# Query, key and value projections regrouped over the engines, a threshold search with experts on partitions, and a gate kept on chip

## The chip, the cores and the metric

The kernel runs on one core of a Trainium2 chip. Its time is device microseconds (us) of one execution, and lower is better. The core has five instruction streams that run side by side and meet at semaphores: TensorE (PE, with its weight loads as PEld), VectorE (DVE), ScalarE (ACT), GpSimd (POOL) and SyncE (SP), which issues most DMAs. Each takes its own instructions in order.

## The reference, cut to what matters

Four pre-norm layers on 4 x 1024 tokens of width 128, in fp32. The parts that the change touches are the two attentions' projections, the routing of the second feed-forward layer and the gated state-space layer:

```python
# L0: q, k = x @ Wq + bq, x @ Wk + bk; 16 heads of 8; rotary: x*cos + rot(x)*sin; v = x @ Wv + bv; softmax attention
# L1 attention: q, k, v = x @ w_qkv.T, no bias, no rotary
# L1 feed-forward: top-1 of 8 experts with a capacity
logits = tokens @ router_w.T
probs = softmax(logits); top1_idx = argmax(probs); top1_prob = max(probs)
order = lexsort((-top1_prob, top1_idx))          # by expert, most probable first
keep = place in the expert's group < capacity    # the others go to expert 0
# L3: state-space layer
xp, z, Bp = split(x @ Win, 3)
...                                              # causal conv of xp, silu, scan -> y
yn = (y - mu) / sqrt(var + 1e-5) * ln_g + ln_b
x = x + (yn * sigmoid(z)) @ Wout * res_scale
```

## The kernel before

The kernel is a row of stages, one function each. A stage allocates its tiles, opens a block with one instruction list per engine, and ends where all engines meet, so the stages' lengths add up. The activations stay on the chip, transposed: 128 features on partitions and 4096 tokens in 8 chunks of 512.

**Projections** (`qkv_stage`, run as `a0_qkv` with biases and rotary, `rope`, and as `a1_qkv` without). It works through 16 items, k = 0 to 15: the query of a chunk (even k) and its key (odd k). Every fp32 result is split into three bf16 parts whose sum is the value: high, the rounded rest, and the rest of that. With rotary an item takes these steps: PE multiplies twice (L408: once plain, once with rotated weights); DVE adds the bias and multiplies with the cosine table, then the same with the sine table (L429, into `t1` and `t2`); POOL adds the two (`full`, L363, semaphore `summed`); ACT rounds it (`high`, L464, into `part[0]`); DVE subtracts (`remain`, L436, into `rest`); ACT rounds the rest (`middle`, L468, `part[1]`); POOL subtracts again (`lo`, L351, `part[2]`); and SP stores the three parts to the DRAM stacks `a_qstk` and `a_kstk` (L379), with three DMAs for a query and four for a key, 128 KB each. The lists interleave items: ACT does `high(k)`, then `middle(k-2)`; POOL `full(k)`, then `lo(k-2)`. Without rotary ACT rounds from PSUM and POOL only does `lo`. The tiles are rings of four items: `high(k)` and `lo(k)` wait until the stores of item k-4 have landed (`stored`). After item 5's stores, SP also fetches the head pairs 0, 1 and 2 of batch 0 back from the stacks, in the forms that attention reads (`fetch_stacks`, four DMAs for each of two heads, L318 to L321): one head after each of items 5 to 10. POOL begins with eight memsets of 32 x 1024 ones (L356).

**Attention** (`attention_stage`) takes 64 head pairs over both layers' batches, fetched by POOL one pair ahead; its first two pairs begin with row maxima alone (PE L604, DVE L693).

**Top-1 routing** (`top1_stage`, `f1r`) needs each expert's capacity-th probability. It searches for it in 14 rounds of base 4 (`dve.Fori`, L1608 to L1626): DVE makes three tries per expert (L1609), compares 128 tokens x 3 x 8 x 32 (L1612), adds up over the tiles (L1615), PE adds over the partitions (L1559), and DVE takes the step (L1617 to L1625). Between the rounds PE turns two tiles of tokens for other use. GpSimd's padding of the gate's weights (L845, L847) comes before the first product of the stage.

**The state-space layer**: `conv_in_stage` writes z to DRAM (L1908), `ssm_stage` scans, `norm_stage` with k = 2 (`m3n`) normalizes, and `ssm_out_stage` (`m3o`) reads z back (L2503), takes its sigmoid (ACT L2511), applies gain and bias (DVE L2521), multiplies (L2526), projects (PE L2541) and adds the result (DVE L2529), in a loop over chunks with two buffers; each chunk's add stands before the next chunk's gain and multiplication on DVE.

## Time and profile before

| | |
|---|---|
| median of three runs | 3428.6 us (3421.51, 3428.60, 3431.22) |
| the profiled execution | 3450.99 us |
| its span, first to last instruction | 3449.3 us |
| PE / DVE / ACT / POOL busy | 78% / 72% / 53% / 29% |
| mean granted TensorE clock | 0.896 |
| `a0_qkv`, `a1_qkv` | 75.2 us, 56.5 us |
| `f1r` | 94.7 us |
| conv, scan, norm, out of the state-space layer | 57.4, 57.6, 38.8, 52.7 us |

Times are microseconds from the start of the span unless marked ns, "x" is a count, and L12 is line 12 of the kernel. An idle time names what ended it. Since a stage ends where all engines meet, a busy share of the whole span tells little here: what counts is, inside a stage, which chain of engines repeats, and how long one turn of it takes.

### The profile page before, as it was taken

How to read it: one execution, taken by the hardware profiler on the slowest of the kernel's cores; microseconds unless marked ns; L12 is line 12 of the kernel's file. 1: busy time of each engine (PE TensorE's matmuls, PEld its weight loads, DVE VectorE, ACT ScalarE, POOL GpSimd, SP SyncE). 2: the span in 40 equal slices, each digit the busy share in tenths (PEclk: the TensorE clock that was granted, in tenths of full speed). 3: DMA queues.
4: the chain of work that ended last, by engine and by line, in shares of the span. 5: the costliest groups of instructions: out<-in, count | busy, mean ns of one | idle time of the engine just before them, and what ended most of it. 6: DMA issues, size and time to landing. Idle time of an engine off the chain costs nothing. (4 is left out here: it accounts for less than half of the span.)

```text
span 3449.3 us, 43078 instructions
## 1 busy us (share of the span) xinstructions
PE 2678.1 (78%) x12690; PEld 960.5 (28%) x12690; DVE 2495.4 (72%) x2926; ACT 1819.0 (53%) x3161; POOL 1003.2 (29%) x1205
## 2 busy tenths in 40 slices
PE   7599999984477669999997418767777778996666
PEld 3122222221155412222221107422232323332222
DVE  6799999954155389999994541579999964446548
ACT  2388888882033248888887104355555531224233
POOL 4222222200635212222220026236777730000000
PEclk9699999997799869999999658888999988998778
DMA  3111111106222311111110402101000000001010
GB/s 95 53 29 24 24 27 23 26 11 153 48 72 65 112 40 24 28 23 24 27 23 23 127 18 70 61 28 39 13 7 13 6 0 0 0 0 60 12 37 25
DMA packets 165673, 128.54 MB, mean 37 GB/s; under 512 B 65341, under 2 KB 138941, under 8 KB 165296
## 3 DMA queue, kind: packets, MB, share of 16 engines
q1 hardware_dynamic: 129520, 85.31, 9.5%
q0 software_dynamic: 34880, 37.57, 4.0%
q10 hardware_dynamic: 1152, 4.19, 0.3%
q8 instruction: 58, 0.95, 0.1%
q14 instruction: 63, 0.52, 0.0%
HBM read 72.80 MB, written 54.09 MB: 37 GB/s over the span
## 5 line engine op out<-in xcount | busy, mean ns | idle before, releaser
L693 DVE TENSOR_REDUCE a_att_mx<-a_att_s 128x2 f32<-128x1024 f32 x1024 | 1204.5, 1218 | 60.1 <-PE a_att_s L604 47.4
L678 ACT ACTIVATE a_att_pt<-a_att_st 128x512 f32<-128x512 f32 x2048 | 1064.5, 603 | 233.3 <-PE a_att_st L630 232.6
L630 PE MATMUL a_att_st<-a_qst,a_kst 50*128 50x512 bf16 x2048 | 623.0, 385 | 62.9 <-ACT a_att_pt L678 51.5
L604 PE MATMUL a_att_s<-a_kst,a_qst 48*128 48x512 bf16 x2048 | 527.1, 400 | 78.1 <-PEq L344 45.2
L617 PE MATMUL a_att_av<-a_att_pt,a_att_vst 128*32 128x512 f32 x4096 | 547.7, 607 | 0.0
L630 PEld LDWEIGHTS a_att_st<-a_qst,a_kst 50*128 50x128 bf16 x2048 | 158.9, 94 | 727.2 <-ACT a_att_pt L678 668.7
L2256 POOL TENSOR_TENSOR g_xn<-m2s_hs,m2s_cb 128x1024 f32<-128x1024 f32 x128 | 300.9, 2356 | 119.0 <-DVE m2s_hs L2223 69.8
L2223 DVE TENSOR_TENSOR_SCAN m2s_hs<-m2s_da,m2s_bps 128x1024 f32<-128x1024 f32 x128 | 292.7, 2287 | 4.4
L531 POOL CAST a_att_mt_in<-a_att_nmax 128x16 bf16<-128x16 f32 x64 | 12.6, 196 | 936.7 <-DVE a_att_nmax L701 936.7
L2139 PE MATMUL m2s_yps<-g_xn,g_ident 128*128 128x512 f32 x512 | 243.8, 599 | 0.9
L2195 ACT COPY m2s_cb<-m2s_cps 128x1024 f32<-128x1024 f32 x128 | 129.5, 1012 | 184.1 <-POOL g_xn L2256 182.1
L604 PEld LDWEIGHTS a_att_s<-a_kst,a_qst 48*128 48x128 bf16 x2048 | 113.1, 94 | 230.9 <-DVE a_att_mx L693 169.9
L2218 DVE TENSOR_TENSOR m2s_bps<-m2s_dtx,m2s_bps 128x1024 f32<-128x1024 f32 x128 | 154.7, 1209 | 3.9 <-POOL m2s_dtx L2242 3.9
L164 POOL MEMSET n_mean_w<- 128x128 f32 x8 | 1.6, 204 | 521.6 <-POOLq L982 232.3
L2190 ACT ACTIVATE m2s_da<-m_dt,m2s_aneg 128x1024 f32<-128x1024 f32 x128 | 147.4, 1151 | 0.0
L2159 PE MATMUL m2s_bps<-m_bcs,m2s_sel 96*128 96x512 bf16 x256 | 79.7, 394 | 83.9 <-DVE m2s_hs L2223 81.3
L1024 ACT ACTIVATE f_sg<-f_gp 128x512 f32<-128x512 f32 x72 | 43.0, 597 | 181.2 <-PE f_cp L1013 181.2
L1036 DVE TENSOR_TENSOR f_h<-f_sg,f_up 128x512 f32<-128x512 f32 x72 | 49.5, 687 | 121.6 <-ACT f_sg L1024 121.6
L2139 PEld LDWEIGHTS m2s_yps<-g_xn,g_ident 128*128 128x128 f32 x512 | 97.2, 191 | 85.6 <-issue 64.1
L617 PEld LDWEIGHTS a_att_av<-a_att_pt,a_att_vst 128*32 128x32 f32 x4096 | 81.0, 108 | 129.8 <-issue 102.6
L271 ACT ACT_TABLE_LOAD x9 | 11.5, 1283 | 183.3 <-PEq L751 64.7
L1258 POOL DMA_INDIRECT f_back<-f_yr,f_to x78 | 74.7, 958 | 88.1 <-DVE f_yr L1452 66.6
(479 smaller groups left out, 3777.7 us busy)
## 6 DMA issues: line engine op xcount, KB each, us to landing
a_kstk<-a_qkv_part SPq DMA_DIRECT2D x64, 128.0 KB
f_xs<-f_sent SPq DMA_DIRECT2D x20, 396.0 KB, 6.1
a_qst<-a_qstk POOLq DMA_DIRECT2D x116, 64.0 KB, 2.3
a_kst<-a_kstk POOLq DMA_DIRECT2D x116, 64.0 KB, 2.4
a_qstk<-a_qkv_part SPq DMA_DIRECT2D x48, 128.0 KB, 2.2
f_sent<-f0r_zero SPq DMA_DIRECT2D x1, 5148.0 KB, 21.9
a_num<-a_att_oev SPq DMA_DIRECT2D x256, 16.0 KB
g_xn<-a_num ACTq DMA_DIRECT2D x8, 512.0 KB, 5.8
```

The source lines that it names most:

```text
L604: mm = pe.matmul(s1[:, cut % 2, h, :], qst[u][64 * h:64 * h + SPECIAL, qt * P:(qt + 1) * P], kst[u][64 * h:64 * h + SPECIAL, kh * CH:(kh + ...
L617: mm = pe.matmul(av[32 * gr:32 * gr + 32, :], vst[u][:, kt, h, :], pt[:, 4 * (kt % 4) + 2 * half + h, :], start=kt == 0, stop=kt == 7)
L630: pe.matmul(st[:, e % 3, :], kst[u][64 * h:64 * h + STACK, kt * P:(kt + 1) * P], qst[u][64 * h:64 * h + STACK, half * CH:(half + 1) * CH], ...
L678: act.activation(pt[:, e % 16, :], st[:, e % 3, :], ACT.Exp, scale=scale).then_inc(exp_done, 1)
L693: dve.tensor_reduce(mx[:, par, 2 * cut:2 * cut + 2], s1[:, cut % 2, :, :], AX.X, ALU.max).then_inc(s1_used, 1)
L2139: mm = pe.matmul(yps[:, f, :], g.ident[:, :], hc[:, k % 4, f * CH:(f + 1) * CH], start=n == 0, stop=n == NS - 1)
L2159: mm = pe.matmul(bps[:, k % 2, f, :], sel[:, n:n + 1].to_broadcast([96, P]), bcs[:, (2 * (q // 2) + f) * CH:(2 * (q // 2) + f + 1) * CH], ...
L2190: act.activation(da[:, k % 4, :], dt[:, q % 2, span(q)], ACT.Exp, scale=aneg[:, q % 2, n:n + 1]).then_inc(da_done, 1)
L2195: act.copy(cb[:, k % 2, :], both(cps[:, :, :])).then_inc(c_copied, 1)
L2218: dve.tensor_tensor(over, dtx[:, q % 2, :], over, ALU.mult).then_inc(dbx_done, 1)
L2223: dve.tensor_tensor_scan(hs[:, k % 3, :], da[:, k % 4, :], over, 0.0, ALU.mult, ALU.add).then_inc(scan_done, 1)
L2256: pool.tensor_tensor(hc[:, k % 4, :], hs[:, k % 3, :], cb[:, k % 2, :], ALU.mult).then_inc(hc_done, 1)
```

## The change

**Projections.** The cosine product is written back into its PSUM bank (L434), and DVE adds it and `t2` (`total`, L447) in POOL's place. With rotary POOL does the first remainder as well as the last (`remain`, L357; `last`, L363). ACT takes `middle(k-1)` ahead of `high(k)`. The three parts lie in one tile, in an order in which a query goes out as one DMA of 128 x 3 x 512 and a key as three. SP fetches head pair 0 only, after item 7, both heads at once; pairs 1 and 2 are fetched by POOL at the start of attention, ahead of its memsets. POOL's first memsets are four of 128 x 1024.

**Threshold search.** The probabilities are turned so that a partition holds one expert and 16 of the tiles (two transposes, one copy); a round is one add, three comparisons of 128 x 256 that accumulate on the way, one product with a matrix that joins the partitions of an expert, one counting comparison and one update, written out 14 times. The 42 offsets are set by GpSimd memsets of 128 x 1 ahead of everything else in the stage.

**State-space layer.** z stays in SBUF (`m3_gate`, 32 KB per partition); its sigmoid is taken at the end of `ssm_stage`; the gain moves into the normalization's last product (`gain`); `ssm_out_stage` is written out for 8 chunks, with two instead of four DVE instructions per chunk ahead of the add, four PSUM banks, and the add two chunks behind.

```diff
-Q_PARTS = [(1, slice(0, HD)), (0, slice(HD, 2 * HD)), (2, slice(2 * HD, 3 * HD))]
-K_PARTS = [(0, slice(0, 2 * HD, 2)), (1, slice(1, 2 * HD, 2)), (2, slice(2 * HD, 3 * HD)), (0, slice(3 * HD, 4 * HD))]
+Q_MOVES = [(slice(0, 3), slice(0, 3 * HD))]
+K_MOVES = [(slice(1, 2), slice(0, 2 * HD, 2)), (slice(0, 1), slice(1, 2 * HD, 2)), (slice(1, 3), slice(2 * HD, 4 * HD))]
...
+                def remain(k):
+                    pool.wait_ge(hi_done, k + 1)
+                    if k >= 4:
+                        pool.wait_ge(lo_done, k - 3)
+                    pool.tensor_tensor(rest[:, k % 4, :], full[:, k % 4, :], hi(k), ALU.subtract).then_inc(rest_done, 1)
...
-                    for h in range(2):
-                        pool.memset(t[64 * h + 32:64 * h + 64, :], 1.0).then_inc(ones_set, 1)
-                pool.wait_ge(ones_set, 8)
+                    pool.memset(t[:, :], 1.0).then_inc(ones_set, 1)
+                pool.wait_ge(ones_set, 4)
+                for k in range(ITEMS):
+                    if rope:
+                        remain(k)
+                        if k >= 1:
+                            last(k - 1)
...
+                        if n == 1:
+                            sp.dma_start(stacks[k % 2][rows, :, cols(k // 2)], part[:, k % 4, parts.start, :]).then_inc(stored[k % 4], 16)
+                        else:
+                            sp.dma_start(stacks[k % 2][rows, :, cols(k // 2)].rearrange("(p r) h t -> (r h) p t", r=HD),
+                                         part[:, k % 4, parts, :]).then_inc(stored[k % 4], 16)
+                    if k == 7:
+                        sp.wait_ge(ones_set, 4)
...
+                        for h in range(2):
+                            fetch_stacks(sp, stacks, qst[0], kst[0], 0, 0, h, first_here)
...
+                    dve.wait_ge(prod, 2 * k + 1)
+                    dve.scalar_tensor_tensor(out=bank(k, 0), in0=bank(k, 0), scalar=col[("bq", "bk")[k % 2]][:, :],
+                                             in1=cos[:, tok], op0=ALU.add, op1=ALU.mult).then_inc(by_cos, 1)
...
+                def total(k):
+                    dve.wait_ge(by_cos, k + 1)
+                    dve.wait_ge(by_sin, k + 1)
+                    if k >= 4:
+                        dve.wait_ge(rest_done, k - 3)
+                    dve.tensor_tensor(full[:, k % 4, :], bank(k, 0), t2[:, k % 2, :], ALU.add).then_inc(summed, 1)
...
@@ attention_stage, POOL
+                for hp in (1, 2):
+                    for h in range(2):
+                        fetch_stacks(pool, stacks, qst[hp], kst[hp], 0, hp, h, ldq[hp])
                 for u in range(4):
                     pool.memset(vst[u][:, :, :, :], 0.0).then_inc(vset, 1)
@@ top1_stage, POOL
+                for k in range(bits):
+                    for j in range(3):
+                        pool.memset(offsets[:, k, j:j + 1], 0.25 ** (k + 1) * (j + 1)).then_inc(offsets_set, 1)
+                pool.wait_ge(offsets_set, 3 * bits)
                 pool.wait_ge(w.here, w.all)
                 found.pad(pool)
@@ top1_stage, PE
+                    pe.wait_ge(counted_here, 3 * (k + 1))
+                    pe.matmul(cnt_ps[:, 0:3], same_w[:, :], parts[:, :], start=True, stop=True).then_inc(counted, 1)
...
+                pe.wait_ge(thr_done, bits + 1)
+                pe.transpose(turned_thr, own_thr[:, :].to_broadcast([P, P]), g.ident[:, :]).then_inc(thr_turned, 1)
@@ top1_stage, DVE
+                for k in range(bits):
+                    dve.wait_ge(thr_done, k + 1)
+                    dve.tensor_scalar(tries[:, :], offsets[:, k, :], own_thr[:, :], None, ALU.add).then_inc(tries_done, 1)
+                    dve.wait_ge(tries_done, k + 1)
+                    for j in range(3):
+                        dve.tensor_scalar(above[:, j, :], by_expert[:, :], tries[:, j:j + 1], None, ALU.is_ge, ALU.add,
+                                          accum_out=parts[:, j:j + 1]).then_inc(counted_here, 1)
                     dve.wait_ge(counted, k + 1)
...
@@ ssm_stage, ACT, its end
+                for b in range(BATCH):
+                    for i in range(2):
+                        z = gate[:, i, b * SEQ:(b + 1) * SEQ]
+                        act.activation(z, z, ACT.Sigmoid).then_inc(opened, 1)
@@ ssm_out_stage, DVE
+                        dve.scalar_tensor_tensor(out=yg[:, c % 4, i, :], in0=yn[:, i, cols(c)], scalar=lb[:, i:i + 1],
+                                                 in1=gate[:, i, cols(c)], op0=ALU.add, op1=ALU.mult).then_inc(gated, 1)
...
+                for c in range(NCH):
+                    weigh(c)
+                    if c >= 2:
+                        add(c - 2)
```

Where the instructions stand, in the changed kernel's lines for "after". First VectorE in `a0_qkv`, from item 4 (`a0_qkv_ps` is the projection in PSUM, `area0` the weights, biases and tables, `a0_v` the values). Before:

```order
L429 SCALAR_TENSOR_TENSOR a0_qkv_t1<-a0_qkv_ps,area0 128x512
L429 SCALAR_TENSOR_TENSOR a0_qkv_t2<-a0_qkv_ps,area0 128x512
L436 TENSOR_TENSOR a0_qkv_rest<-a0_qkv_full,a0_qkv_part0 128x512
L429 SCALAR_TENSOR_TENSOR a0_qkv_t1<-a0_qkv_ps,area0 128x512
L429 SCALAR_TENSOR_TENSOR a0_qkv_t2<-a0_qkv_ps,area0 128x512
L419 TENSOR_TENSOR a0_v<-a0_qkv_v,area0 128x512
L436 TENSOR_TENSOR a0_qkv_rest<-a0_qkv_full,a0_qkv_part0 128x512
```

After:

```order
L434 SCALAR_TENSOR_TENSOR a0_qkv_ps<-a0_qkv_ps,area0 128x512
L439 SCALAR_TENSOR_TENSOR a0_qkv_t2<-a0_qkv_ps,area0 128x512
L447 TENSOR_TENSOR a0_qkv_full<-a0_qkv_ps,a0_qkv_t2 128x512
L434 SCALAR_TENSOR_TENSOR a0_qkv_ps<-a0_qkv_ps,area0 128x512
L439 SCALAR_TENSOR_TENSOR a0_qkv_t2<-a0_qkv_ps,area0 128x512
L447 TENSOR_TENSOR a0_qkv_full<-a0_qkv_ps,a0_qkv_t2 128x512
L427 TENSOR_TENSOR a0_v<-a0_qkv_v,area0 128x512
```

The remainder, which had both inputs in SBUF, is gone from VectorE; a sum with one input in PSUM stands in its place, directly behind the products it adds. GpSimd's list at the same place read `full`, last remainder, `full`, last remainder; it now reads first remainder of k, last remainder of k-1.

Second, VectorE in `f1r`, one round of the search and what stands before it (`f1r_pm` the probabilities by token, `f1r_cnt` the counts in PSUM). Before, in a loop:

```order
L1603 SCALAR_TENSOR_TENSOR f_block_k<-g_ones 128x23
L1604 TENSOR_SCALAR f1r_count_k<-f_block_k 128x23
L1608 UNCONDITIONAL_BRANCH
L1609 TENSOR_TENSOR f1r_tries<-f1r_inc,f1r_thr 128x24
L1611 REGISTER_ALU
L1612 TENSOR_TENSOR f1r_above<-f1r_pm,f1r_tries 128x768
L1615 TENSOR_REDUCE f1r_parts<-f1r_above 128x24
L1617 SCALAR_TENSOR_TENSOR f1r_passed<-f1r_cnt,f1r_inc 128x24
L1621 TENSOR_REDUCE f1r_step_sum<-f1r_passed 128x8
L1624 TENSOR_SCALAR f1r_inc<-f1r_inc 128x24
L1625 TENSOR_TENSOR f1r_thr<-f1r_thr,f1r_step_sum 128x8
L1608 REGISTER_ALU
```

After, written out:

```order
L1631 SCALAR_TENSOR_TENSOR f_block_k<-g_ones 128x23
L1632 TENSOR_SCALAR f1r_count_k<-f_block_k 128x23
L1633 MEMSET f1r_own_thr 128x1
L1636 COPY f1r_by_expert<-f1r_gate_row 128x256
L1640 TENSOR_SCALAR f1r_tries<-f1r_offsets,f1r_own_thr 128x3
L1643 TENSOR_SCALAR f1r_above,f1r_parts<-f1r_by_expert,f1r_tries 128x256 x3
L1646 TENSOR_SCALAR f1r_passed,f1r_passes<-f1r_cnt 128x3
L1649 SCALAR_TENSOR_TENSOR f1r_own_thr<-f1r_passes,f1r_own_thr 128x1
```

The comparison of 768 elements and the separate reduction have become three instructions of 256 elements, and four small ones have become two.

## Rows read from the trace of the kernel before

**Rows 1.** Windows: length, then busy us (count) of PE, PEld, DVE, ACT, POOL, granted clock, DMA share, GB/s.

```profile
35.60:110.80 75.20, 40.41 (x128) 20.93 (x129) 45.07 (x56) 18.24 (x33) 51.02 (x41) 0.80 0.37 112
110.80:148.00 37.20, 20.75 (x72) 3.57 (x73) 36.55 (x35) 2.55 (x5) 3.68 (x13) 0.50 0.03 8
190.00:500.00 310.00, 297.58 (x2012) 71.47 (x2013) 298.52 (x284) 268.95 (x520) 79.05 (x176) 1.00 0.11 26
1161.90:1218.40 56.50, 26.85 (x96) 15.81 (x96) 15.84 (x24) 17.58 (x32) 25.83 (x24) 0.71 0.48 149
3268.20:3320.90 52.70, 26.22 (x32) 8.10 (x32) 23.08 (x40) 13.14 (x12) 0.00 (x0) 0.63 0.23 80
```

**Rows 2.** Waits in `a0_qkv`, 35 to 111 us: total, times, longest.

```profile
ACT a_qkv_part L464 <- POOL a_qkv_full L363: 53.0, 14, 18.5
```

**Rows 3.** Timeline of `a0_qkv`: start, us, engine, line, operation, count, idle before.

```profile
35.65 7.93 POOL L356 MEMSET a_kst<- 32x1024 bf16 x8 [20.90 <-POOLq L156]
...
39.48 0.75 DVE L429 SCALAR_TENSOR_TENSOR a_qkv_t<-a_qkv_ps,area 128x512 f32<-128x512 f32 x1 [0.87 <-PE a_qkv_ps L408]
...
43.67 2.50 POOL L363 TENSOR_TENSOR a_qkv_full<-a_qkv_t 128x512 f32<-128x512 f32 x2
...
44.97 1.41 DVE L429 SCALAR_TENSOR_TENSOR a_qkv_t<-a_qkv_ps,area 128x512 f32<-128x512 f32 x2 [1.71 <-POOL a_qkv_full L363]
...
62.48 1.71 POOL L363 TENSOR_TENSOR a_qkv_full<-a_qkv_t 128x512 f32<-128x512 f32 x1
...
64.80 0.61 ACT L468 CAST a_qkv_part<-a_qkv_rest 128x512 bf16<-128x512 f32 x1
65.49 1.15 POOL L351 TENSOR_TENSOR a_qkv_part<-a_qkv_rest,a_qkv_part 128x512 bf16<-128x512 f32 x1 [1.30 <-ACT a_qkv_part L468]
65.55 1.64 DVE L436 TENSOR_TENSOR a_qkv_rest<-a_qkv_full,a_qkv_part 128x512 f32<-128x512 f32 x1
```

**Rows 4.** Waits in `a1_qkv`, 1161 to 1219 us.

```profile
ACT a_qkv_part L464 <- DMA a_kstk<-a_qkv_part: 16.7, 6, 4.5
```

**Rows 5.** Timeline of `a1_qkv`, ScalarE: item 4's rounding.

```profile
1173.96 0.58 ACT L464 CAST a_qkv_part<-a_qkv_ps 128x512 bf16<-128x512 f32 x1 [3.84 <-DMA a_qstk<-a_qkv_part]
```

**Rows 6.** The stores' line, L379: issue ns min/median/max, and landing.

```profile
L379 SPq DMA_DIRECT2D a_kstk<-a_qkv_part x64: 427/529/778, 54.2 to 1217.6; - x64
...
DMA to landing us min/median/max: 1.9/2.2/3.3
```

**Rows 7.** Timeline of `f1r`: first try, the step after a count, first row behind the search.

```profile
1956.08 0.18 DVE L1609 TENSOR_TENSOR f1r_tries<-f1r_inc,f1r_thr 128x24 f32<-128x24 f32 x1 [0.20 <-DVE f1r_count_k L1604]
...
1964.47 0.18 DVE L1617 SCALAR_TENSOR_TENSOR f1r_passed<-f1r_cnt,f1r_inc 128x24 f32<-128x24 f32 x1 [0.71 <-PE f1r_cnt L1559]
...
2020.81 0.43 DVE L1628 TENSOR_TENSOR f1r_t<-f1r_pm,f1r_thr 128x256 f32<-128x256 f32 x1 [0.21 <-DVE f1r_thr L1625]
```

**Rows 8.** Groups by line: a tensor-scalar instruction of VectorE; busy, mean ns.

```profile
L1946 DVE TENSOR_SCALAR m3i_acc<-m3i_xb,g_area 128x512 f32 x16 | 7.0, 481 | 4.5 <-ACT m_xs L1965 4.5
```

**Rows 9.** Timeline at the program's start: memsets of one column on GpSimd.

```profile
0.32 0.10 POOL L2813 MEMSET const-bfloat16-1.0<- 128x1 bf16 x1
0.35 0.10 POOL L2813 MEMSET const-uint8-127<- 128x1 uint8 x1
```

**Rows 10.** Timeline of norm `m3n` and of `m3o`, where z is read back.

```profile
3229.66 1.28 ACT L271 ACT_TABLE_LOAD   x1 [13.35 <-PEq L2291]
...
3262.85 4.87 DVE L238 TENSOR_TENSOR m_xs<-m_xs,m3n_row 128x512 f32<-128x512 f32 x8 [2.21 <-PE m3n_row L205]
...
3273.20 1.28 ACT L2511 ACT_TABLE_LOAD   x1 [19.00 <-DMA m3o_zt<-m_z]
3274.49 2.00 ACT L2511 ACTIVATE m3o_sg<-m3o_zt 128x1024 f32<-128x1024 f32 x2
...
3288.08 1.98 PE L2541 MATMUL m3o_ps<-m3o_yg,g_area 128*128 128x512 f32 x4 [2.44 <-DVE m3o_yg L2526]
...
3298.09 3.78 PE L2541 MATMUL m3o_ps<-m3o_yg,g_area 128*128 128x512 f32 x4 [2.44 <-DVE m3o_yg L2526]
```

301 lines of the change are left out of this document (130 added, 171 removed).

## The prediction, as put on record before the changed kernel ran

> **What bounds the kernel now.** I first read the table of windows by stage [rows 1]: stages end where all engines meet, so a saving inside one shortens the whole by as much, and each edit is priced in its own stage. Then, per stage, the waits and the timeline. Attention itself is bound by TensorE at full clock (297.58 of 310.00 us) and its code hardly changes. In `a0_qkv` no engine is busy for more than 51.02 of 75.20 us. The longest wait is ScalarE's for GpSimd's sum, 53.0 us [rows 2]: a loop over engines, to be seen in the timeline [rows 3]. GpSimd's `full` (1.71) releases ScalarE's `high`, `middle` of two items back (0.61) stands behind that, and `lo` (1.15) behind that; only then comes the next `full`: 1.71 + 0.61 + 0.61 + 1.15 with short handoffs is 4.1 us per item, 16 times. In `a1_qkv` ScalarE waits for the landing of stores, for the keys alone 16.7 us [rows 4]. The search runs from 1956.08 to 2020.81 [rows 7], 64.7 us, 4.62 a round, in one chain through DVE and PE. In `m3o` the chain per chunk passes DMA, ACT, DVE, PE and DVE, and little overlaps; ScalarE's first wait there, counted from inside the norm, ends with z's landing at 3273.20, 5 us into the stage [rows 10].
>
> **A: `a0_qkv`.** Per item DVE now does two products (1.41 the pair), a sum (about 0.68, the pair's second half plus the same class as the uncontended remainder) and half a value copy (0.34): 2.4. GpSimd does two remainders. None of its rows is such a first remainder; the nearest are `full` alone, 2.50 for two, so 1.25, and `full` beside a DVE remainder with both inputs in SBUF, 1.71, in which case that remainder takes 1.64 [rows 3]. The DVE pair from PSUM at 44.97 ran inside the 2.50 and neither was stretched. In the changed kernel every DVE instruction of this stage has at most one tensor input in SBUF, as that pair had, so I take 1.25; with `last` at 1.15 that is 2.4. The loop is now first remainder 1.25, `middle` 0.61, `high` 0.61 and three handoffs of some 0.05: **2.6 us per item**; GpSimd's last remainder runs beside ScalarE. PE's 40.41 us make 2.5 an item, partly at the lower clock, so PE is next in line. The sum: the first item's sine product still starts at 39.48; plus 0.75 and the sum 0.69, `high(0)` starts at 41.0. The memsets, 7.93 for eight, halve and end at 39.6, ahead of it. Fifteen turns end at 80.0; the last item's chain is 0.6 + 1.25 + 0.6 + 1.15 and handoffs, 3.9; three key stores at 0.53 to issue [rows 6] 1.8; leaving 0.4. The eight fetches behind item 7, at 0.53 or a little more 4.5 us of SP, hold up item 8's store, for which item 12 waits: its slack is about 2, so 2.5 is added. End at 88.6 instead of 110.8: **-22**. Bounds: remainders at 1.71 with `last` (loop 3.06), -15; loop at the engines' own 2.4 and no hold-up, -28.
>
> **B: `a1_qkv`.** A ring of four items turns through `high` 0.58, remainder 0.69, `middle` 0.61, `lo` 1.15, handoffs 0.3, issue and landing. Issue was three or four DMAs per item plus four fetches, and SP had little air; it is one or three now. Landing was 1.9 to 3.3 [rows 6]; the joined stores carry two or three times the bytes, so I take the upper part: 3.3 + 1.6 + 3.3 is 8.2, **2.0 per item**. Item 4's rounding started at 1173.96 [rows 5]; four memsets less and one query DMA instead of three bring it to 1171. Eleven items later 1193; the eight fetches hold up 4; the last item's chain 3.3, its stores 1.8, leaving 0.4: 1202.8 against 1218.4, **-15.6**. Bounds: 1.7 per item and nothing held up, -23; 2.6 per item, -9.
>
> The fetches of pairs 1 and 2 move to GpSimd at the start of attention: 16 DMAs, some 9 us, ahead of its memsets. All of GpSimd's list queues behind them, and pair 1's row maxima wait for the first eight. In that stretch GpSimd works 3.68 of 37.20 us, while DVE is busy for 36.55 [rows 1] and reaches pair 1 only halfway: zero; without that cover at most 9 per layer.
>
> **C: the search.** A round: tries 0.2; three accumulating comparisons of 256 elements, of which no row exists; the count over PE 0.71 [rows 7]; two small steps 0.44; another 0.05. The nearest row by size is 0.43 for 256 elements in a tensor-tensor instruction [rows 7]; by kind, 0.48 for 512 [rows 8]. I take the former, as accumulation is something extra: three overlapping a little, 1.1. A round is 2.5, fourteen 34.7: 30.0 less. To be paid: turning the threshold back over PE, about 0.71 and two small handoffs, 1.4; the copy of the turned probabilities less four memsets, 0.1; 42 memsets of GpSimd ahead of the padding for which the stage's first product waits: 0.03 apart or 0.10 long [rows 9], 1.4 to 4.2; I take 2.5. **-26**. Bounds: comparisons as by kind (0.3 each), -32; a full second pass in each, as the old compare and reduce, 2.5 for the three, -6.
>
> The Trainium skill, "VectorE: DVE Perf Modes", section on the perf-mode tier table, says that a tensor-scalar instruction on fp32 in SBUF runs at twice the rate of a tensor-tensor one. The 0.48 for 512 elements agrees; whether accumulation keeps the rate no row here shows. By the rule the term would be -32. [...]
>
> **D: the state-space layer.** Eight sigmoids, 2.00 for two and a table load 1.28, take 9.3 us on ScalarE, which idles 13.35 at that place [rows 10]: hidden; without cover up to 9. The normalization's 16 products go from 0.61 to 0.66 each (4.87 for eight; 1.41 for two with a scalar [rows 3]): +1. In `m3o` DVE needs three instructions of 0.66 per chunk, 2.0. PE needs 3.78 per chunk at 1.2 GHz and 1.98 at 2.4 GHz [rows 10]. It enters after a pause, at the lower level; in `a0_qkv` and `a1_qkv`, also entered after a pause, the granted clock came to 0.80 and 0.71 of full speed [rows 1], so it rose early there. So: 1.4 to the first product, 3.8, 2.7 for a chunk that changes over, then six at DVE's pace less the two that wait ready, about 10, and the last add 0.9: 18.8 against 52.7, -34. With the +1, **-33**. The bound is 1.2 GHz throughout: 1.4 + 8 x 3.6 + 0.8, 31, so -21.
>
> **The sum**: -22 - 15.6 - 26 - 33 = -96.6. The profiled execution took 3450.99 us, 22.4 above the median; it would take 3354.4, and the median becomes 3428.6 - 96.6 = **3332 us**.
>
> **Rivals.**
> 1. *Stores bound both projections.* A joined store lands late, since it moves 384 KB where 128 KB took up to 3.3, and the ring waits at every item: A at 3.0, B at 2.6 per item, 6.5 + 6.5 lost: 3345. For: the DMA share was already 0.48 in `a1_qkv`. Against: SP issues far less.
> 2. *`m3o` stays at 1.2 GHz*: 12 lost, 3344. For: it ran mostly there before. Against: it will be fed without pauses.
> 3. *Accumulation costs a second pass*: 20 lost, 3352.
> 4. *Slower than before*: attention loses the clock. DVE has 18 rows a pair, so the 284 rows of the 310 us are 15.8 pairs, 19.6 us each, with PE busy for 96% of it; at 1.2 GHz instead of 2.4 it takes about 19 more. The place is the entry into attention, which PE reaches at 0.50 [rows 1] and from which it must rise; if more than five of the 64 pairs fall short, all that was won is gone, and ten give 3428.6 - 96.6 + 190 = 3522. For: the entry's first pair waits for GpSimd's fetches now. Against: they land long before, and 190 to 500 us shows 1.00.
>
> **How the numbers follow.** The forecast holds 0.70, rival 1 0.10, rival 2 0.09, rival 3 0.06, rival 4 0.05 (0.03 over the line, 0.02 at five pairs, where nothing is left). All lower bounds at once (-28, -23, -32, -33) give 3313, all upper ones (-15, -9, -6, -21) 3378; they are independent, so their squares add: about 11 below and 25 above, and the runs spread by some 5 each way. Range **3314 to 3362**, which takes in rivals 1 to 3 alone. A measurement of this kernel tells about 0.3%, 10 us, from no change: faster 0.95, within 0.02, slower 0.03.
>
> **What would show it.** `a0_qkv` some 53 us with GpSimd rows of 1.25 and 1.15 and one item every 2.6; rows of 1.7 would refute A. In `a1_qkv` some 41 us, ScalarE's waits for landings mostly gone but for one near item 12; rival 1 shows as a wait at every item. In the search a round of 2.5 with comparison rows near 0.4; `f1r` near 69 us. `m3o` near 19 us with a clock above 0.8; rival 2 shows 3.8 per chunk. ScalarE's sigmoids end before DVE's last sum in the scan. The forecast is wrong if the attention windows change by more than a few us, or if a stage not named here moves.

## The result and the profile after the change

| | before | after |
|---|---|---|
| median of runs, us | 3426.2 (3421.5 to 3431.2, 4 runs) | 3328.5 (3326.8 to 3354.9, 4 runs) |
| ratio, 95% interval | | 0.9732 [0.9704, 0.9761] |
| profiled execution / its span | 3450.99 / 3449.3 | 3326.78 / 3325.0 |
| TensorE's granted clock, mean | 0.896 | 0.908 |

The kernel became 98 us faster by the medians, 92 ± 10 us by the ratio; 3332 us were forecast. The profiled executions differ by 124 us, which is more than the change brought: 30.6 us of it lie in the first expert stage, `f0r` and `f0`, whose code is the same in both (below). By stage, from the first instruction of one to that of the next, in us:

| stage | before | after | difference | forecast |
|---|---|---|---|---|
| `a0_qkv` | 75.1 | 52.6 | -22.5 | -22 |
| attention and output, first layer | 702.2 | 703.2 | +1.0 | 0 |
| `f0r`, `f0` (unchanged code) | 305.9 | 275.3 | -30.6 | 0 |
| `a1_qkv` | 56.5 | 43.9 | -12.6 | -15.6 |
| attention and output, second layer | 702.6 | 702.2 | -0.4 | 0 |
| `f1r`, `f1` | 253.1 | 226.8 | -26.3 | -26 |
| `m3s` | 57.8 | 59.6 | +1.8 | 0 |
| `m3n`, `m3o` | 91.5 | 57.5 | -33.9 | -33 |

The four stages that the change speeds up give -95.3, with `m3s` -93.5. The windows of the changed kernel answer to [rows 1]; columns as there, the last row being `m3o`:

```profile
34.67:87.31 52.64, 37.18 (x128) 20.22 (x129) 37.20 (x56) 18.73 (x33) 39.99 (x36) 0.86 0.45 143
87.31:111.00 23.69, 12.74 (x44) 2.27 (x44) 23.01 (x22) 1.48 (x2) 12.45 (x29) 0.50 0.19 51
190.00:500.00 310.00, 297.27 (x2012) 71.64 (x2016) 298.59 (x284) 268.57 (x520) 76.36 (x170) 1.00 0.11 25
1109.86:1153.72 43.86, 24.47 (x96) 14.14 (x96) 15.66 (x24) 17.48 (x32) 21.91 (x20) 0.81 0.54 170
3180.00:3198.92 18.92, 16.68 (x32) 7.03 (x32) 16.23 (x24) 0.00 (x0) 0.00 (x0) 0.83 0.00 0
```

In `a0_qkv` GpSimd is busy 11 us less than in [rows 1] and no engine is busy for more than 40.0 of 52.6 us. In the attention's entry, 87.31 to 111.00, GpSimd works 12.45 us where the kernel before had 3.68 [rows 1]: the 16 moved fetches. DVE stays at 23.01 of 23.69 us there, and from attention's start to ScalarE's first exponential it is 36.0 us in both kernels (110.77 to 146.79, 87.31 to 123.32), so they are hidden, as the step on the fetches had it. Attention itself still has a granted clock of 1.00.

The item of `a0_qkv`, in the timeline of all engines (start, us, engine, line, operation, tiles, count, idle before), TensorE and SyncE left out; it answers to [rows 3]:

```profile
57.68 0.61 ACT L474 CAST a_qkv_part<-a_qkv_full 128x512 bf16<-128x512 f32 x1
...
58.37 1.16 POOL L357 TENSOR_TENSOR a_qkv_rest<-a_qkv_full,a_qkv_part 128x512 f32<-128x512 f32 x1
...
58.69 0.69 DVE L447 TENSOR_TENSOR a_qkv_full<-a_qkv_ps,a_qkv_t 128x512 f32<-128x512 f32 x1
...
59.49 1.15 POOL L363 TENSOR_TENSOR a_qkv_part<-a_qkv_rest,a_qkv_part 128x512 bf16<-128x512 f32 x1
...
59.56 0.62 ACT L478 CAST a_qkv_part<-a_qkv_rest 128x512 bf16<-128x512 f32 x1 [1.27 <-POOL a_qkv_rest L357]
...
60.08 0.61 ACT L474 CAST a_qkv_part<-a_qkv_full 128x512 bf16<-128x512 f32 x1
...
60.77 1.16 POOL L357 TENSOR_TENSOR a_qkv_rest<-a_qkv_full,a_qkv_part 128x512 f32<-128x512 f32 x1
```

From one first remainder (58.37) to the next (60.77) it is 2.40 us, and the way leads through the loop that the forecast named: first remainder 1.16, handoff 0.03, `middle` (59.56), `high` 0.52 behind its start (60.08), 0.61 for `high`, handoff 0.08. It is 2.4 and not 2.6 because the remainder takes 1.16 and not 1.25, and because ScalarE starts `high` 0.52 behind `middle`, not 0.61. GpSimd's last remainder runs beside ScalarE and ends at 60.64, 0.13 before GpSimd may go on. VectorE, with two products, a sum and half a value copy an item, needs 2.4 us as well (its sums start at 53.90, 58.69 and 63.48, two items apart): it is as close to the limit as the loop. The rest of the stage's length is a wait for stores. The waits of ScalarE in the two projections (total us, times, longest), which answer to [rows 2] and [rows 4]:

```profile
ACT a_qkv_part L478 <- POOL a_qkv_rest L357: 20.3, 16, 1.3
ACT a_qkv_part L474 <- DMA a_qstk<-a_qkv_part: 3.8, 1, 3.8
...
ACT a_qkv_part L474 <- DMA a_kstk<-a_qkv_part: 11.4, 6, 3.2
ACT a_qkv_part L474 <- DMA a_qstk<-a_qkv_part: 6.7, 3, 5.7
```

The first two are of `a0_qkv`, the last two of `a1_qkv`. The longest of each stage, 3.8 and 5.7 us, is item 12's wait behind the eight fetches. The other eight in `a1_qkv` are the ring of four.

The search, VectorE's and TensorE's rows of one round; they answer to [rows 7]:

```profile
1896.85 0.23 DVE L1640 TENSOR_SCALAR f1r_tries<-f1r_offsets,f1r_own_thr 128x3 f32<-128x3 f32 x1
1897.12 0.48 DVE L1643 TENSOR_SCALAR_CACHE_REDUCE f1r_above<-f1r_by_expert,f1r_tries 128x256 f32<-128x256 f32 x1
1897.52 0.08 DVE L1643 DVE_READ_ACCUMULATOR f1r_above<-f1r_by_expert,f1r_tries 128x1 f32 x1
1897.52 0.47 DVE L1643 TENSOR_SCALAR_CACHE_REDUCE f1r_above<-f1r_by_expert,f1r_tries 128x256 f32<-128x256 f32 x1
...
1898.46 0.59 PE L1586 MATMUL f1r_cnt<-f1r_parts,f1r_same 128*128 128x3 f32 x2 [1.51 <-DVE f1r_above L1643]
...
1899.48 0.23 DVE L1640 TENSOR_SCALAR f1r_tries<-f1r_offsets,f1r_own_thr 128x3 f32<-128x3 f32 x1
```

A round is 2.63 us (1896.85 to 1899.48; 4.62 before, 2.5 forecast). Each comparison is an instruction of 0.48 us and a read of the accumulator of 0.08, and they start 0.40 apart: 1.28 for the three against the 1.1 of the forecast.

### The profile page after: what moved, and what is told of

It is laid out like the page before. It is cut to its first block and busy times, and to the rows that moved or that the text cites. A ratio compares the mean times of both kernels' runs of the same rounds, so it can differ in the third digit from the quotient of the medians.

```text
span 3325.0 us, 42836 instructions
## 1 busy us (share of the span) xinstructions
PE 2664.8 (80%) x12693; PEld 959.3 (29%) x12693; DVE 2465.1 (74%) x2953; ACT 1815.3 (55%) x3157; POOL 1006.7 (30%) x1271
## 5 line engine op out<-in xcount | busy, mean ns | idle before, releaser
L708 DVE TENSOR_REDUCE a_att_mx<-a_att_s 128x2 f32<-128x1024 f32 x1024 | 1204.8, 1219 | 62.0 <-PE a_att_s L619 49.7
L541 POOL CAST a_att_mt_in<-a_att_nmax 128x16 bf16<-128x16 f32 x64 | 12.6, 198 | 914.6 <-DVE a_att_nmax L716 914.6
```

The source lines that it names most:

```text
L708: dve.tensor_reduce(mx[:, par, 2 * cut:2 * cut + 2], s1[:, cut % 2, :, :], AX.X, ALU.max).then_inc(s1_used, 1)
```

## The experiments

Stages of every kernel's profiled execution, as above, in us; "att" is attention with its output stage:

| kernel | `a0_qkv` | att 1 | `f0` | `a1_qkv` | att 2 | `f1` | `m3s` | `m3n`+`m3o` |
|---|---|---|---|---|---|---|---|---|
| before | 75.1 | 702.2 | 305.9 | 56.5 | 702.6 | 253.1 | 57.8 | 91.5 |
| after | 52.6 | 703.2 | 275.3 | 43.9 | 702.2 | 226.8 | 59.6 | 57.5 |
| after_again | 53.0 | 721.6 | 272.8 | 42.9 | 702.2 | 226.8 | 59.6 | 57.6 |
| proj_only | 54.0 | 719.5 | 274.8 | 43.8 | 711.7 | 251.9 | 59.6 | 87.6 |
| search_only | 75.2 | 702.4 | 276.3 | 56.5 | 721.2 | 226.6 | 59.2 | 93.0 |
| ssm_only | 75.5 | 702.4 | 275.0 | 56.8 | 702.7 | 252.8 | 61.7 | 57.6 |
| cos_in_sbuf | 56.2 | 703.8 | 273.2 | 43.7 | 701.5 | 227.0 | 59.6 | 57.5 |
| stores_apart | 54.3 | 702.4 | 273.7 | 44.7 | 702.0 | 228.0 | 57.8 | 58.7 |
| fetch_spread | 51.2 | 702.7 | 273.6 | 41.2 | 702.6 | 226.4 | 59.6 | 57.6 |
| ring8 | 49.8 | 702.8 | 273.7 | 38.9 | 719.6 | 226.7 | 59.6 | 57.5 |
| ring8_act | 49.7 | 703.8 | 273.8 | 36.7 | 701.1 | 228.0 | 61.9 | 57.7 |
| count_by_reduce | 52.1 | 702.7 | 272.8 | 43.7 | 702.4 | 236.5 | 59.6 | 57.5 |
| add_at_once | 54.8 | 702.1 | 273.8 | 43.0 | 702.1 | 227.0 | 59.6 | 71.0 |
| fill_tail | 49.4 | 703.9 | 273.4 | 38.3 | 703.4 | 226.8 | 59.6 | 57.6 |

Where a stage's code is the same, the table shows its scatter: `a0_qkv` of the changed kernel 52.1 to 54.8, `a1_qkv` 42.9 to 43.9, attention 701 to 704 but 712 to 722 in five of 28 cases, `f0` 273 to 276 in 13 executions and 305.9 in one.

### The three parts alone

**proj_only** has all of the change but the search and the state-space layer, in short:

```diff
+LO, HI, MID = (0, 2), (1, 1), (2, 0)
...
+                    dve.tensor_tensor(full[:, k % 4, :], bank(k, 0), t2[:, k % 2, :], ALU.add).then_inc(summed, 1)
...
+                for hp in (1, 2):
+                    for h in range(2):
+                        fetch_stacks(pool, stacks, qst[hp], kst[hp], 0, hp, h, ldq[hp])
```

> The kernel before with the projections, the joined stores and the moved fetches alone; search and state-space layer as before. Theory 1 (every part acts in its own stage; the 30 us by which the first transformer block's expert layers were shorter in the one profiled execution of the changed kernel are scatter of that execution): a0_qkv near 52.6 and a1_qkv near 43.9 us, attention and its output +1.0 in the first block, 35 us less than before, so about 3391. Theory 2 (the expert stage behind the first attention, whose code is unchanged, is lastingly shorter by some 30 us, and some other part gained that much less): 60 to 65 us less, about 3363, with that stage near 275 us here too.

**search_only** has the search alone:

```diff
+                        dve.tensor_scalar(above[:, j, :], by_expert[:, :], tries[:, j:j + 1], None, ALU.is_ge, ALU.add,
+                                          accum_out=parts[:, j:j + 1]).then_inc(counted_here, 1)
```

> The kernel before with the turned search alone. Theory 1: the routed expert stage falls from 253 to 227 us, all in the search; 26 us less, about 3400; the norm and the expert stages behind it unchanged. Theory 2 (the experts behind the search hide part of it, or another stage moves with it): less than 15 us or more than 35.

**ssm_only** has the state-space layer's change alone:

```diff
+                        act.activation(z, z, ACT.Sigmoid).then_inc(opened, 1)
...
+                        dve.scalar_tensor_tensor(out=yg[:, c % 4, i, :], in0=yn[:, i, cols(c)], scalar=lb[:, i:i + 1],
+                                                 in1=gate[:, i, cols(c)], op0=ALU.add, op1=ALU.mult).then_inc(gated, 1)
```

> The kernel before with the state-space layer's change alone. Theory 1: norm and output stage together 57.5 instead of 91.5 us; m3s between 57.8 and 59.6; 32 to 34 us less, about 3393. If m3s is longer by 1.8 us because of the eight sigmoids, it is 59.6 here too; if that was TensorE's clock at the end of that stage, the rows that grew are matmuls, and m3s may be 57.8 here. Rival (sum right by compensation): the three parts alone add up to less than 85 or more than 110 us.

Measured against the kernel before, whose median was 3436.0 in these comparisons: proj_only 0.9893 [0.9855, 0.9931], search_only 0.9921 [0.9893, 0.9949], ssm_only 0.9879 [0.9848, 0.9911]. By the ratios that is 37, 27 and 42 us less, 106 together, ± 20 when the half intervals are added by squares; the whole change gave 92 ± 10 by its ratio. By the medians it is 40, 33 and 47, or 121, against 98: more than the 110 that the expectation allowed. The kernel before had a median of 3436 in this comparison and of 3421 to 3426 in the others, so the whole times are too coarse to settle the sum. The stages settle it. Against the row of before, proj_only saves 21.1 and 12.7 us in the two projections, search_only 26.5 in `f1`, ssm_only 33.9 in `m3n` and `m3o`: 94.2 together, where the whole change saved 95.3 in these stages. So the parts add up, each in its own stage, and theory 1 holds for all three. The `f0` stage is near 275 us in each of them, in two of which its code and that of all that precedes it is that of the kernel before. The 305.9 us of the profiled execution of before were thus scatter and no gain of the change. They more than account for the 22 us by which that execution stood above its median.

The 1.8 us of `m3s` are not the sigmoids: proj_only, which has none, shows 59.6 too, and stores_apart, which has them, shows 57.8. The granted clock differs, over the whole stage (0.82 where it takes 57.8 us, 0.78 at 59.6, and 0.74 at the 61.7 and 61.9 of ssm_only and ring8_act) and most in its last 24 us. Windows of that stretch, proj_only, then stores_apart (columns as in [rows 1]):

```profile
3171.00:3195.10 24.10, 15.01 (x24) 4.36 (x22) 17.30 (x13) 2.27 (x3) 0.04 (x1) 0.65 0.00 1
```

```profile
3114.00:3137.50 23.50, 13.26 (x29) 4.33 (x28) 18.21 (x14) 11.19 (x11) 0.00 (x0) 0.75 0.00 0
```

ScalarE works 11.19 us in the shorter and 2.27 in the longer one. The sigmoids are hidden, as forecast: in the changed kernel ScalarE still idles 5.81 us before the norm's table load.

### Why the item of `a0_qkv` fell to 2.4 us

**cos_in_sbuf:**

```diff
-            t2, full = s.sb("t2", [P, 2, CH]), s.sb("full", [P, 4, CH])
+            t1, t2, full = s.sb("t1", [P, 2, CH]), s.sb("t2", [P, 2, CH]), s.sb("full", [P, 4, CH])
...
-                    dve.scalar_tensor_tensor(out=bank(k, 0), in0=bank(k, 0), scalar=col[("bq", "bk")[k % 2]][:, :],
+                    dve.scalar_tensor_tensor(out=t1[:, k % 2, :], in0=bank(k, 0), scalar=col[("bq", "bk")[k % 2]][:, :],
...
-                    dve.tensor_tensor(full[:, k % 4, :], bank(k, 0), t2[:, k % 2, :], ALU.add).then_inc(summed, 1)
+                    dve.tensor_tensor(full[:, k % 4, :], t1[:, k % 2, :], t2[:, k % 2, :], ALU.add).then_inc(summed, 1)
```

> The changed kernel, but the cosine product is written to SBUF again, so DVE's sum has both inputs there. Theory 1 (a DVE instruction with two inputs in SBUF and GpSimd's remainders stretch each other, as the two kinds did in the kernel before: 1.71 against 1.25 and 1.64 against 0.69 us): GpSimd's first remainder rises from 1.16 to 1.5 to 1.7, DVE's sum from 0.69 to 1.2 or more, the item from 2.41 to 3.0 or more, a0_qkv from 52.6 to 62 or more; a1_qkv stays at 43.9. Theory 2 (keeping the product in PSUM buys nothing, the loop is shorter only because both remainders stand on one engine and ScalarE no longer lags two items): rows unchanged, a0_qkv 52.6 within 1.

The groups by line and shape from 50 to 80 us (busy, mean ns, idle before) of cos_in_sbuf:

```profile
L363 POOL TENSOR_TENSOR a_qkv_part<-a_qkv_rest,a_qkv_part 128x512 bf16<-128x512 f32 x10 | 16.1, 1614 | 0.0
L357 POOL TENSOR_TENSOR a_qkv_rest<-a_qkv_full,a_qkv_part 128x512 f32<-128x512 f32 x10 | 11.6, 1156 | 4.1 <-ACT a_qkv_part L476 4.1
L449 DVE TENSOR_TENSOR a_qkv_full<-a_qkv_t 128x512 f32<-128x512 f32 x11 | 10.1, 919 | 1.0
```

and of the changed kernel:

```profile
L363 POOL TENSOR_TENSOR a_qkv_part<-a_qkv_rest,a_qkv_part 128x512 bf16<-128x512 f32 x11 | 12.7, 1158 | 0.0
L357 POOL TENSOR_TENSOR a_qkv_rest<-a_qkv_full,a_qkv_part 128x512 f32<-128x512 f32 x11 | 12.7, 1156 | 6.2 <-ACT a_qkv_part L474 5.3
...
L447 DVE TENSOR_TENSOR a_qkv_full<-a_qkv_ps,a_qkv_t 128x512 f32<-128x512 f32 x11 | 7.6, 692 | 1.0
```

With both inputs in SBUF the same sum takes 0.92 instead of 0.69 us on average, and GpSimd's last remainder 1.61 instead of 1.16. The mechanism of theory 1 is shown, and the choice of 1.25 rather than 1.71 in term A rested on it. Its size was expected wrongly: the first remainder, which was to rise to 1.5 or more, stayed at 1.16, an item takes 2.69 us (1.16 and 1.61 with GpSimd never idle), not 3.0, and the stage 56.2, not 62. Theory 1's numbers failed, while theory 2 failed on the rows. In the timeline it is the instruction that starts second that gets longer: at 62.54 the sum starts first and keeps its 0.69, and the remainder from 62.62 takes 1.62; at 64.21 a first remainder starts first and keeps its 1.15, and the sum from 64.64 takes 1.27. The program's time doesn't tell it from the changed kernel (0.9728 [0.9695, 0.9761]). The bulk of the 22 us comes from the stage's other edits: the sum on VectorE instead of GpSimd, both remainders on GpSimd, and `middle` ahead of `high`. No run took these apart; that the loop became 2.4 us through them is read from the rows.

### What bounds the stores

**stores_apart:**

```diff
-                            sp.dma_start(stacks[k % 2][rows, :, cols(k // 2)].rearrange("(p r) h t -> (r h) p t", r=HD),
-                                         part[:, k % 4, parts, :]).then_inc(stored[k % 4], 16)
+                            sp.dma_start(stacks[k % 2][r, :, cols(k // 2)], part[:, k % 4, j, :]).then_inc(stored[k % 4], 16)
```

> The changed kernel with seven stores a chunk again (three of a query item, four of a key item) where it has four. Theory 1 (issue is the scarce part): with about 0.53 us to issue each, 1.6 us more of SyncE per chunk, so the backlog behind the eight fetches drains more slowly: a0_qkv 1.5 to 3 us longer, a1_qkv 2 to 6 us longer. Theory 2 (a joined store lands so late, 3.0 to 4.7 us against 1.9 to 3.3, that it gives back what it saves): a0_qkv within 1, a1_qkv unchanged or up to 2 us shorter.

Measured 3324.4 us, 0.9703 [0.9675, 0.9731]; `a0_qkv` 54.3 and `a1_qkv` 44.7, both within 1 us of what the same code of the changed kernel gave in other executions. Against the changed kernel's first execution `a0_qkv` is 1.7 us longer, as theory 1 has it but inside that stage's scatter, and `a1_qkv` 0.8, nearer to theory 2; the total can't decide. The joined stores buy some 2 us a stage at most, and may buy nothing. The rows show why. Separate stores, line 388 of stores_apart in `a0_qkv` (issue ns min/median/max; landing), then the joined ones of the changed kernel:

```profile
L388 SPq DMA_DIRECT2D a_kstk<-a_qkv_part x32: 334/525/773, 49.0 to 89.1; - x32
L388 SPq DMA_DIRECT2D a_qstk<-a_qkv_part x24: 319/447/997, 46.5 to 86.9; - x24
...
DMA to landing us min/median/max: 1.9/2.1/2.7
```

```profile
L389 SPq DMA_DIRECT2D a_qstk<-a_qkv_part x8: 365/366/496, 45.6 to 84.1; - x8
L389 SPq DMA_DIRECT2D a_kstk<-a_qkv_part x8: 470/472/476, 49.5 to 86.4; - x8
...
DMA to landing us min/median/max: 2.5/2.9/4.4
```

A joined query store is issued in 0.37 us where three took 1.34, and the joined stores land 0.8 us later by the medians, so of some 1.0 us saved 0.8 is given back. In `a1_qkv`, where the ring waits for landings, the medians are 2.1 us apart and 3.3 joined: there the later landing takes all of it.

**fetch_spread:**

```diff
-                        for h in range(2):
-                            fetch_stacks(sp, stacks, qst[0], kst[0], 0, 0, h, first_here)
+                    if k in (9, 12):
+                        fetch_stacks(sp, stacks, qst[0], kst[0], 0, 0, (9, 12).index(k), first_here)
```

> The changed kernel with the eight fetches of pair 0 in two groups of four, one head behind the stores of item 9, the other behind those of item 12. Theory 1 (the waits of 3.8 us in a0_qkv and 5.7 us in a1_qkv at item 12 come from SyncE's 4.8 us of issuing in one piece): these waits fall below 1 and 2.5, a0_qkv 49 to 50.5, a1_qkv 40 to 42, 5 to 7 us less in all. Theory 2 (the waits come from the transfers of the fetches on the DMA engines, or the ring is bound by landing anyway): the wait moves behind the new places and both stages stay within 1 us.

Measured 3317.8 us, 0.9682 [0.9654, 0.9710], all four runs between 3316.8 and 3318.8. The long waits fell from 3.8 to 1.8 and from 5.7 to 3.3 us, the stages to 51.2 and 41.2: theory 1's mechanism, with 4.1 us of the 5 to 7 expected, since four fetches in one piece still hold up a store.

**ring8** (with the fetches spread):

```diff
-        rest, part = s.sb("rest", [P, 4, CH]), s.sb("part", [P, 4, 3, CH], BF16)
+        rest, part = s.sb("rest", [P, 4, CH]), s.sb("part", [P, 8, 3, CH], BF16)
-        hi, mid, lo = (lambda k, i=i: part[:, k % 4, i[k % 2], :] for i in (HI, MID, LO))
+        hi, mid, lo = (lambda k, i=i: part[:, k % 8, i[k % 2], :] for i in (HI, MID, LO))
```

> As the kernel with the fetches spread, and the rounded parts in a ring of eight items where it has four, with a semaphore for each. Theory 1 (a1_qkv is bound by the landing of stores through its ring of four): ScalarE's waits for stores vanish, the item falls from 2.4 towards the 1.2 to 1.4 us that ScalarE and GpSimd need, a1_qkv 28 to 34 us, a0_qkv unchanged beside the spread kernel, since GpSimd's and DVE's 2.4 bound that one. Theory 2 (the DMA engines themselves bound a1_qkv, 896 KB a chunk): a1_qkv within 3 us of the spread kernel, and the last stores land late. In all about 3313 by theory 1, 3322 by theory 2.

ScalarE's waits for stores are gone but for 0.9 us, and `a1_qkv` runs at 1.3 us an item (GpSimd's pairs of remainders start at 1117.37 and 1120.03, two items apart). Yet the stage took 38.9 us and not 28 to 34. Its timeline:

```profile
1117.37 2.27 POOL L363 TENSOR_TENSOR a_qkv_part<-a_qkv_rest,a_qkv_part 128x512 bf16<-128x512 f32 x2 [0.34 <-ACT a_qkv_part L478]
...
1120.03 2.27 POOL L363 TENSOR_TENSOR a_qkv_part<-a_qkv_rest,a_qkv_part 128x512 bf16<-128x512 f32 x2 [0.39 <-ACT a_qkv_part L478]
...
1129.90 2.26 POOL L363 TENSOR_TENSOR a_qkv_part<-a_qkv_rest,a_qkv_part 128x512 bf16<-128x512 f32 x2 [0.89 <-ACT a_qkv_part L478]
...
1142.80 1.05 SPq L389 DMA_DIRECT2D a_kstk<-a_qkv_part  x1
```

The last remainder is done at 1132.2 and SyncE issues until 1143.9. The engines' work is no longer the bound, the queue of stores is. Each theory had half: the ring did bound the items, and behind it stood the issuing. The median was 3327.0 us (3316.9 to 3334.9), 0.9701 [0.9672, 0.9730], where 3313 was expected: three of its five runs lie 10 us or more above its fastest, and the profiled one has an attention of 719.6 us.

**ring8_act** asked which of the two, SyncE or the DMA engines, sets the pace of that queue:

```diff
+                places = (9, 12) if rope else (13, 15)
...
+                    if k in places:
+                        fetch_stacks(act, stacks, qst[0], kst[0], 0, 0, places.index(k), first_here)
```

> As ring8, but the eight fetches of pair 0 are issued by ScalarE (in a0_qkv one head behind its work for item 9, one behind item 12; in a1_qkv behind items 13 and 15), so SyncE only stores. Theory 1 (in ring8, a1_qkv no longer waits for buffers: the engines are done at 1133.0, and SyncE still issues until 1143.9, 4.8 us of it fetches): a1_qkv 34 to 36 us instead of 38.9, a0_qkv 49 to 50.5 instead of 50.1, since ScalarE has half its time free there; about 4 us less than ring8. Theory 2 (the DMA engines, at a share of 0.64 to 0.82 in that stretch, set the pace of SyncE's issuing): a1_qkv 38 to 39 as before, with longer issues of stores.

`a0_qkv` is 49.7 us; the expectation counts ring8's 50.1 up to ScalarE's first instruction, the table's 49.8 up to TensorE's. `a1_qkv` is 36.7 us, between the two: 2.2 of 4.8 us came back. The rest went into longer issues of stores: the 16 strided ones took 12.7 us of SyncE in ring8 and 17.9 here. The median is 3323.4 us, 0.9705 [0.9668, 0.9742], 3.6 less than ring8's in another comparison and not told apart from it. Windows (columns as in [rows 1]) and two timeline rows of ring8_act:

```profile
1130.00:1135.00 5.00, 0.00 (x0) 0.00 (x0) 1.29 (x2) 1.34 (x3) 2.98 (x3) 0.75 0.86 267
1135.00:1140.00 5.00, 0.00 (x0) 0.00 (x0) 0.00 (x0) 0.00 (x0) 0.24 (x1) 0.50 0.85 279
```

```profile
1129.63 2.65 SPq L387 DMA_DIRECT2D a_kstk<-a_qkv_part  x2
...
1137.60 2.97 SPq L387 DMA_DIRECT2D a_kstk<-a_qkv_part  x2
```

Two such stores took mostly 1.2 us to issue in `a0_qkv` and take 1.33 to 3.02 in `a1_qkv`, 2.65 and 2.97 in the two rows, at a DMA share of 0.85. So it seems that in `a1_qkv` SyncE and the DMA engines are near their limits together; no run changed the load of the DMA engines alone.

### The search and the output stage

**count_by_reduce:**

```diff
-                        dve.tensor_scalar(above[:, j, :], by_expert[:, :], tries[:, j:j + 1], None, ALU.is_ge, ALU.add,
-                                          accum_out=parts[:, j:j + 1]).then_inc(counted_here, 1)
+                        dve.tensor_scalar(above[:, j, :], by_expert[:, :], tries[:, j:j + 1], None, ALU.is_ge).then_inc(cmp_done, 1)
+                    dve.wait_ge(cmp_done, 3 * (k + 1))
+                    dve.tensor_reduce(parts[:, :], above[:, :, :], AX.X, ALU.add).then_inc(counted_here, 3)
```

> The changed kernel, with each of the search's three comparisons written without accumulation and one reduction over the 768 results behind them. It tells what of the 0.475 us of an accumulating comparison of 256 elements is the accumulation. Theory 1 (accumulation slows it): plain comparisons 0.2 to 0.3 us, the reduction 0.8 to 1.0, the round near 2.6 as now, the routed stage 226.8 within 4 us. Theory 2 (a comparison of 256 elements costs 0.4 us or more either way): comparisons 0.4 us or more, the round 3.1 to 3.4, the stage 7 to 12 us longer.

Its groups by line (busy, mean ns, idle before):

```profile
L1646 DVE TENSOR_REDUCE f1r_parts<-f1r_above 128x3 f32<-128x768 f32 x13 | 12.4, 953 | 1.3
L1644 DVE TENSOR_SCALAR f1r_above<-f1r_by_expert,f1r_tries 128x256 f32<-128x256 f32 x37 | 10.9, 349 | 0.4
```

A comparison without accumulation takes 0.349 us, with it 0.475 (and 0.08 to read the accumulator): it does slow the instruction, but costs a third, not a second pass. Successive ones start 0.26 us apart without it and 0.40 with it. The stage is 236.5 us, 9.7 longer; 3336.0 us, 0.9742 [0.9703, 0.9782]. The rows lie between the theories' and the stage went theory 2's way.

**add_at_once:**

```diff
                     weigh(c)
-                    if c >= 2:
-                        add(c - 2)
-                add(NCH - 2)
-                add(NCH - 1)
+                    add(c)
```

> The changed kernel, but in m3o DVE adds chunk c right behind its two products instead of two chunks later; the rest of the state-space change stays. Theory 1 (a good part of the 34 us comes from the two-chunk lag that lets DVE and TensorE overlap): per chunk 1.3 of products, 1.1 to 2.0 of matmuls behind the second product, 0.7 of adding and handoffs 0.2, 3.3 to 4.1 us instead of 2.0, so m3o 8 to 15 us longer. Theory 2 (the gain is the fetch of z, the sigmoids and the affine step that left the stage): m3o within 2 us.

`m3n` and `m3o` took 71.0 us, 13.5 longer: theory 1. Its timeline gives 3.48 us a chunk at full clock, where the changed kernel needs 1.99 (3189.38 to 3191.37 below):

```profile
3190.08 0.75 DVE L2538 SCALAR_TENSOR_TENSOR g_xT<-m3o_ps,g_area,g_xT 128x512 f32<-128x512 f32 x1 [1.42 <-PE m3o_ps L2555]
3190.74 1.41 DVE L2532 SCALAR_TENSOR_TENSOR m3o_yg<-m_xs,g_area,m_gate 128x512 f32<-128x512 f32 x2
...
3193.56 0.75 DVE L2538 SCALAR_TENSOR_TENSOR g_xT<-m3o_ps,g_area,g_xT 128x512 f32<-128x512 f32 x1 [1.41 <-PE m3o_ps L2555]
```

```profile
3189.38 0.74 DVE L2538 SCALAR_TENSOR_TENSOR g_xT<-m3o_ps,g_area,g_xT 128x512 f32<-128x512 f32 x1
...
3191.37 0.74 DVE L2538 SCALAR_TENSOR_TENSOR g_xT<-m3o_ps,g_area,g_xT 128x512 f32<-128x512 f32 x1
```

So 13.5 of the 34 us come from the lag of two chunks. The other 20 are left, by subtraction, for z, the sigmoids, the affine step that left the stage and the four PSUM banks; no run took these apart. The median was 3339.0 us, 0.9747 [0.9708, 0.9786].

### The scatter, and a faster version

In five of the 28 attentions of the table it was 9 to 19 us longer than in the rest, with attention and projections as before the change (search_only) and with them changed. In all five the clock falls in the last two pairs, where DVE has no more maxima and TensorE pauses for ScalarE. Windows of the end of the first attention: after_again (721.6 us), then the first profiled execution of the same kernel (703.2 us); columns as in [rows 1]:

```profile
710.00:720.00 10.00, 9.91 (x68) 2.31 (x64) 9.86 (x9) 8.44 (x17) 0.00 (x0) 1.00 0.06 10
720.00:730.00 10.00, 7.95 (x47) 1.61 (x46) 1.62 (x3) 8.67 (x17) 0.41 (x2) 0.90 0.06 9
730.00:740.00 10.00, 9.21 (x36) 1.28 (x36) 0.00 (x0) 5.97 (x12) 0.00 (x0) 0.50 0.00 0
```

```profile
710.00:720.00 10.00, 9.05 (x64) 2.09 (x60) 7.29 (x8) 8.79 (x17) 0.41 (x2) 1.00 0.02 2
720.00:730.00 10.00, 7.91 (x51) 1.85 (x51) 0.00 (x0) 8.76 (x18) 0.00 (x0) 1.00 0.05 8
730.00:740.00 10.00, 7.99 (x51) 1.76 (x48) 0.00 (x0) 8.90 (x18) 0.00 (x0) 1.00 0.01 2
```

The same work goes on at 1.00 (2.4 GHz) in one and falls to 0.50 (1.2 GHz) in the other, where it stays for the rest of the attention. In the 10 us in which the one fell TensorE was busy for 7.95 us, in the other for 7.91, and from 700 us to the fall none of its pauses was longer than 0.67 us: what decides between them is not seen in these rows.

**fill_tail** (ring8_act, and in the last two of each attention's 32 pairs):

```diff
+                            else:
+                                if kt == 0 and half == 0:
+                                    pe.wait_ge(s1_used, CUTS * NPAIR)
+                                pe.matmul(s1[:, half, 0, :], qst[u][0:SPECIAL, kt * P:(kt + 1) * P],
+                                          kst[u][0:SPECIAL, half * CH:(half + 1) * CH], start=True, stop=True)
```

> As ring8_act, with one added product per half block in the last two of the 64 pairs of each attention (32 a layer, 48 by 128 by 512, written to the score banks that nothing reads any more), where TensorE otherwise works only 7.8 to 8.1 of 10 us. Theory 1 (the 9 to 19 us by which attention is longer in some executions, in which the granted clock falls to 0.50 over the last two pairs, come from TensorE's pauses there): the granted clock stays at 1.00 to the end of both attentions, each attention 702 to 704 us, all runs within some 8 us of each other near 3313, and the median 8 to 12 us below that of ring8_act. Theory 2 (the clock falls there for a reason that the pauses don't set): runs from 3313 to 3339 as for ring8_act.

**after_again** is the changed kernel itself, beside fill_tail; ring8_act below is from an earlier comparison:

> The changed kernel itself once more. Theory 1 (the forecast's median is right, not helped by a lucky draw): runs between 3324 and 3360 in two groups some 16 to 26 us apart, by whether the clock fell at the end of an attention; ratio 0.970 to 0.976; a0_qkv 52.6 within 1.5, a1_qkv 43.9 within 1, routed stage 226.8, norm and output stage of the state-space layer 57.5. Theory 2 (one term of the sum was right only in that execution): one of these stages off by more than 3 us.

| kernel | runs, us |
|---|---|
| ring8_act | 3312.8, 3312.9, 3317.2, 3329.7, 3332.0, 3338.6 |
| after_again | 3323.2, 3323.5, 3324.3, 3324.7, 3339.9, 3343.0 |
| fill_tail | 3314.4, 3314.6, 3316.7, 3318.0, 3318.6 |

The rows of fill_tail at the same place:

```profile
720.00:730.00 10.00, 8.80 (x59) 2.17 (x56) 0.00 (x0) 8.71 (x18) 0.00 (x0) 1.00 0.04 8
730.00:740.00 10.00, 8.75 (x57) 2.01 (x56) 0.00 (x0) 8.78 (x18) 0.00 (x0) 1.00 0.01 2
```

The clock stays, the attentions are 703.9 and 703.4 us, and the runs lie within 4.2 us, as theory 1 has it. The added products have a price: from DVE's last maximum to TensorE's last product it is 40.4 us, against 39.1 in every attention that kept the clock without them, 1.3 us an attention, and the fastest run is 1.6 us above that of ring8_act. But of the 41 runs of the changed kernel and its other variants 11 were more than 8 us above the fastest of their kernel, so five without one could be chance at 0.73 to the fifth, 1 in 5. Beside ring8 and ring8_act alone, with 6 of 11 runs, it would be 1 in 50; yet stores_apart, fetch_spread and add_at_once, which fill nothing, had no long run in four each. That the pauses of TensorE are the cause is likely, not settled. The median is 3316.7, 6.7 below that of ring8_act, where 8 to 12 were expected; 0.9686 [0.9661, 0.9711], against 0.9719 [0.9692, 0.9745] for the changed kernel beside it: the intervals overlap. The changed kernel's own repetition, median 3324.5 with four runs at 3323 to 3325 and two some 16 and 19 us above, had every changed stage within 1.0 us of the first execution: theory 1 there too. fill_tail and fetch_spread, the latter a change of a few lines, both beat it by some 8 to 10 us by their medians, and can't be told apart.

## Why the prediction was right, step by step

- **What bounds the kernel, and that stages add.** Right. proj_only, search_only and ssm_only each changed their own stage, and the stages' savings, 94.2 us, agree with the whole's 95.3. Taking the profiled execution's 22.4 us as a shift of its own that the change doesn't touch was right too; it was the long `f0`, whose cause stays open: TensorE is busy there for 199 us in the one and 195 us in the other execution, the rest is more waiting, and no experiment repeated it.
- **A, `a0_qkv`, -22.** Came at -22.5 (-22.1 in after_again), with two small errors that cancel; that they do so to within half a microsecond is luck. The loop is the one that was named, first remainder, `middle`, `high`, but it takes 2.4 and not 2.6 us, as the remainder takes 1.16 and `high` starts 0.52 behind `middle`: 15 turns, 3 us less. The eight fetches hold item 12 up by 3.8 us, where 2.5 was added, and two other items wait 0.6 us for stores. The price of GpSimd's remainders, 1.16 where 1.25 was taken, and the reason given for not taking 1.71, were borne out by cos_in_sbuf. One reading of [rows 3] was off: the remainder of 1.64 at 65.55 ran beside `lo` (65.49, 1.15), not beside the `full` of 1.71, which ended at 64.19. The choice didn't hang on it, since in both cases the stretched instruction met one with two inputs in SBUF.
- **B, `a1_qkv`, -15.6.** Came at -12.6 (-13.6 in after_again). The term that was mis-sized is the turn of the ring, 2.0 us an item. Item 4's rounding started 8.8 us into the stage (9.1 forecast); from there to item 15 it took 29.5 us, where 11 items of 2.0 and a hold-up of 4 make 26; behind item 15 came 5.6, where 5.5 was forecast. Without the 4 an item is 2.3. ring8 shows that it was the ring, as the step said, though without its waits the stage is only 2.3 us shorter than fetch_spread's, as SyncE's issuing is next. stores_apart shows why the joined stores shortened the turn so little: they give back in landing what they save in issuing.
- **The fetches moved to GpSimd: zero.** Right: the attention's entry, 36.0 us to the first exponential, and its 702 to 703 us are unchanged.
- **C, the search, -26.** Came at -26.3. A round is 2.63 and not 2.5, as the three comparisons take 1.28 and not 1.1: 1.8 us more. The 42 memsets took 1.45 us (one row, 0.03 each) and not 2.5. The rule of the Trainium skill, "VectorE: DVE Perf Modes", section on the perf-mode tier table, holds for the plain comparison: 0.349 us for 256 elements here, 0.481 for 512 in [rows 8], so 256 more elements cost 0.13, where a tensor-tensor instruction pays 0.26 (0.43 for 256 in [rows 7], 0.69 for 512 in L447). With accumulation 256 elements take 0.475, so the rule's -32 was not to be had.
- **D, the state-space layer, -33.** Came at -33.9. `m3o` took 18.9 us, 18.8 were forecast, and TensorE's clock changed over in the second chunk, as it said. The microsecond added for the normalization didn't come: `m3n` took 38.7 us, 38.8 before. The sigmoids are hidden. `m3s` was 1.8 us longer by its clock, without the change's doing.
- **The rivals.** Rival 1 is partly there, in `a1_qkv` alone: at 2.3 us, not 2.6. Rivals 2 and 3 are refuted by the 0.83 clock of `m3o` and by count_by_reduce. Rival 4 looked at the wrong end: the entry to attention holds, but the clock does fall in some executions, of the kernel with and without the change, at the exit, over the last two pairs. Between an attention's first 110 and its last 80 us the clock was 1.00 in all 28 of the table, so the long run of pairs on which its price rested was never touched.
- **The range**, 3314 to 3362, held both medians, 3328.5 and 3324.5. The stages' sum, -93.5 with `m3s`, is within 3 us of the forecast's -96.6; that the first median lies 3.5 us from 3332 is partly luck, as single executions of this kernel scatter over 28 us and the ratio is known to 10 us.

## What to carry to other kernels

Price a loop over several engines by who waits for whom, one item at a time; what an engine can do beside the longest chain doesn't count, and two instructions in a row on one engine can start closer together than the first one's length, as `middle` and `high` here. Before joining small transfers, ask what the ring waits for, issue plus landing: a larger transfer lands later. And look for the places where a tuned kernel's scatter arises: here the clock, when it falls at the end of an attention where TensorE pauses, costs 9 to 19 us, and products that nobody reads filled the pauses for 1.3 us an attention; the five runs with them lie within 4.2 us of each other.

## What the runs showed of the hardware

- VectorE with both inputs in SBUF and GpSimd's elementwise instruction stretch each other, 0.69 to 0.92 and 1.16 to 1.61 us on average, and in the rows looked at it is the one that starts second that gets longer; with one input in PSUM neither is stretched.
- An accumulating comparison of 256 fp32 elements takes 0.475 us and a separate read of 0.08, and the next starts 0.40 behind it; the plain one takes 0.349, and the next starts 0.26 behind it.
- The same stretch of the same program, the last two pairs of an attention, kept 2.4 GHz in 23 of 28 cases and fell to 1.2 GHz in five, which costs 9 to 19 us of 702.
- The same strided store took 0.58 us to issue in `a0_qkv` and about 1.5 (2.97 for two) in the stretch of `a1_qkv` where the DMA engines' share was 0.85.
